# Six attention nodes as one flow of 48 units, with float32r stacks made by the projections

## The chip, the cores and the metric

The kernel runs on one core of one Trainium2 chip. The metric is the device time of one execution in microseconds; the time before is the median of three. The core has five engines that matter here, each working through its own instructions in order: TensorE (PE, with its weight loads shown as PEld), VectorE (DVE), ScalarE (ACT), GpSimd (POOL) and SyncE (SP, which issues DMAs). They wait for each other through semaphores.

## The reference, cut to what matters

The whole program is eight sublayers over x of shape (8, 256, 128). Only the feed-forward of layer 0 is touched. It is six attention nodes with heads of 16 elements, each reading up to three earlier nodes:

```python
for c in range(6):
    nsrc = min(c + 1, 5); snode = c - nsrc
    eq, ek, ev = lind + nsrc - 1, lind, lind + nsrc // 2
    q = ew[c, 0] * (nodes[c - 1] @ We[eq] + be[eq])
    k = ew[c, 1] * (nodes[snode] @ We[ek] + be[ek])
    v = ew[c, 2] * (nodes[snode + nsrc // 2] @ We[ev] + be[ev])
    # mha: H = 8 heads; softmax(qh kh^T / sqrt(16)) vh, then @ Wo
    nodes[c] = act_w[c] * mha(q, k, v, Wq[c], Wk[c], Wv[c], Wo[c]) + q
    lind += nsrc
return layernorm(nodes[5], ln_g, ln_b)
```

Batch n of node c reads only batch n of earlier nodes.

## The kernel before, in words

Layer 0's feed-forward is the functions `l0f_*` (lines 748 to 866). `l0f_sp` loads the weights, `l0f_dve` normalises x (`ln_dve`), then for each of the six nodes c there are three stages with a barrier of all five engines between them:

1. Projections, for all 8 batches at once in 512-column chunks: `cols_pe` (L671) makes q with columns as tokens (`qcol`) and, in `tcol`, k; `rows_pe` (L681) multiplies by Wq and Wk and puts rows of tokens into `Qf` and `Kf`; then v goes the same way into V. `l0f_empty` evacuates the banks, alternately on ACT and DVE (L696, L703, L704, L712), and multiplies the edge weight `ew` in at that point.
2. Attention, batch after batch (`Heads.events` gives the order, `att_pool`, `att_pe`, `att_act`, `att_dve` carry it out). There are 4 pairs of heads in a batch. POOL splits the float32 q and k of `Qf` and `Kf` into three bf16 parts each, set side by side in `Qst` and `Kst`, 6 x 16 entries for a head (L281 to L300). PE transposes these stacks (K and T events, L337), ACT and DVE evacuate them (L455, L469). A: PE scores of a pair (L379, contraction over 97 rows), of which DVE takes the row maxima (L479). After each half of the heads DVE writes the negated maxima as two bf16 columns into `Qst` (L489, L491), PE transposes this stack again (X event) and ACT evacuates it as `QpT` (L459). B: PE makes the transposed scores with the maxima in the contraction (L392, 99 rows), ACT takes the exponential (L451). V: PE multiplies by v (L406), O: ACT copies the result (L446), R: PE turns it (L416) and DVE divides by the sum (L501, L504).
3. Output: PE turns O (L663), evacuated into `tcol`; PE multiplies by Wo (L671); DVE makes `nodes` (L819).

Banks 0 and 1 hold the scores of A, 2 and 3 those of B, 4 the product with v. Banks 5 to 7 are taken in turn by everything else (`turning`), and a job waits until the job three before it has been evacuated. A pair's A waits for the maximum of the pair before, its B for the exponential of the pair before.

After the sixth node PE turns the result back (L663) and DVE does a second layer norm (L231 on). The DVE and POOL work at the edges of the stage is in L231 to L237, L253 to L259 and L846. Layer 1's attention (L971 to L1126) and layer 3's feed-forward (L1664 to L1898) are not changed; they already use float32r operands.

## Time and profile before

| | us |
|---|---|
| median of 3 runs | 2422.3 (2419.29 to 2423.67) |
| the profiled execution's own time | 2432.78 |
| its span | 2431.0 |
| layer 0's feed-forward, from its first instruction to the second layer norm | 231.3 to 1074.65 |

| engine | busy us | share of the span |
|---|---|---|
| PE | 1654.4 | 68% |
| PEld | 1154.3 | 47% |
| DVE | 1533.2 | 63% |
| ACT | 948.1 | 39% |
| POOL | 523.8 | 22% |

Busy time is the time in which an engine works on an instruction; waiting for a semaphore is not busy. L12 is line 12 of the kernel. Where a row says what ended an engine's idle time, that is inferred from semaphore events. Times are in us from the start of the span unless marked ns.

### The profile page before, as it was taken

How to read it: one execution, taken by the hardware profiler on the slowest of the kernel's cores; microseconds unless marked ns; L12 is line 12 of the kernel's file. 1: busy time of each engine (PE TensorE's matmuls, PEld its weight loads, DVE VectorE, ACT ScalarE, POOL GpSimd, SP SyncE). 2: the span in 40 equal slices, each digit the busy share in tenths (PEclk: the TensorE clock that was granted, in tenths of full speed). 3: DMA queues.
4: the chain of work that ended last, by engine and by line, in shares of the span. 5: the costliest groups of instructions: out<-in, count | busy, mean ns of one | idle time of the engine just before them, and what ended most of it. 6: DMA issues, size and time to landing. Idle time of an engine off the chain costs nothing. (4 is left out here: it accounts for less than half of the span.)

```text
span 2431.0 us, 39616 instructions
## 1 busy us (share of the span) xinstructions
PE 1654.4 (68%) x16146; PEld 1154.3 (47%) x16146; DVE 1533.2 (63%) x2306; ACT 948.1 (39%) x1175; POOL 523.8 (22%) x746
## 2 busy tenths in 40 slices
PE   1784787887877787853898889334882367630598
PEld 0562555555565555531565556223651334320497
DVE  5664563656556563666666766685658767569565
ACT  0563473755547473741333333122662047510010
POOL 6321341415143341401000000014300233000121
PEclk9997898999989998985999999756996669855599
DMA  1013000000000000001000000000000000000143
GB/s 56 4 10 73 3 1 1 1 1 2 1 1 1 1 1 1 1 1 53 1 1 1 1 1 1 9 20 1 2 2 9 26 1 1 18 34 17 38 125 103
DMA packets 61355, 38.28 MB, mean 16 GB/s; under 512 B 37572, under 2 KB 53380, under 8 KB 60420
## 3 DMA queue, kind: packets, MB, share of 16 engines
q1 hardware_dynamic: 60164, 34.55, 5.1%
q8 instruction: 127, 2.08, 0.4%
q0 software_dynamic: 1024, 1.32, 0.2%
q14 instruction: 40, 0.33, 0.0%
HBM read 32.71 MB, written 3.15 MB: 15 GB/s over the span
## 5 line engine op out<-in xcount | busy, mean ns | idle before, releaser
L451 ACT ACTIVATE Pt<-bank 128x1024 f32<-128x1024 f32 (+1 forms) x384 | 366.3, 954 | 302.7 <-PE bank L392 301.5
L479 DVE TENSOR_REDUCE Mx<-bank 128x4 f32<-128x1024 f32 x256 | 312.8, 1222 | 101.9 <-PE bank L379 101.7
L379 PE MATMUL bank<-KT,QT 97*128 97x256 bf16 (+2 forms) x1536 | 198.1, 281 | 87.1 <-DVE Mx L479 70.5
L392 PE MATMUL bank<-QpT,KT 99*128 99x256 bf16 (+2 forms) x1536 | 186.8, 267 | 37.1 <-ACT QpT L459 33.5
L406 PE MATMUL bank<-Pt,V 128*32 128x256 f32 (+1 forms) x3072 | 198.9, 378 | 9.6 <-ACT Pt L451 9.6
L337 PE MATMUL bank<-identb,Qst 128*128 128x128 bf16 x2304 | 174.8, 232 | 19.2 <-POOL Qst L300 14.1
L455 ACT COPY QT<-bank 128x1024 bf16<-128x1024 bf16 x144 | 139.4, 1027 | 112.1 <-PE bank L337 112.1
L469 DVE COPY KT<-bank 128x1024 bf16<-128x1024 bf16 x144 | 98.8, 691 | 132.7 <-PE bank L337 132.4
L281 POOL CAST Kst<-Kf 128x256 bf16<-128x256 f32 x72 | 28.6, 398 | 706.8 <-PE bank L337 403.2
L337 PE MATMUL bank<-identb,Kst 128*128 128x128 bf16 x1152 | 94.6, 233 | 117.9 <-POOL Kst L290 68.5
L459 ACT COPY QpT<-bank 128x1024 bf16<-128x1024 bf16 x144 | 145.0, 1007 | 72.6 <-PE bank L337 72.6
L337 PEld LDWEIGHTS bank<-identb,Qst 128*128 128x128 bf16 x2304 | 150.7, 104 | 39.9 <-issue 16.5
L379 PEld LDWEIGHTS bank<-KT,QT 49*128 49x128 bf16 (+1 forms) x1536 | 89.5, 98 | 163.4 <-DVE Mx L479 84.9
L392 PEld LDWEIGHTS bank<-QpT,KT 51*128 51x128 bf16 (+1 forms) x1536 | 107.5, 98 | 69.7 <-ACT QpT L459 47.9
L337 PEld LDWEIGHTS bank<-identb,Kst 128*128 128x128 bf16 x1152 | 74.2, 105 | 135.4 <-issue 69.6
L406 PEld LDWEIGHTS bank<-Pt,V 128*32 128x32 f32 x3072 | 81.6, 111 | 84.1 <-issue 40.1
L501 DVE RECIPROCAL Rden<-bank 128x16 f32<-128x16 f32 x96 | 24.8, 258 | 146.6 <-PE bank L416 146.6
L1120 DVE RECIPROCAL st<-bank 128x256 f32<-128x256 f32 x64 | 111.9, 1749 | 7.8 <-PE bank L1033 7.7
L663 PE MATMUL bank<-ident,Qf 128*128 128x128 f32 x64 | 14.3, 415 | 148.6 <-POOLq L162 96.1
L1095 DVE TENSOR_TENSOR qk_lo<-bank,qk_hi 128x512 fp32r<-128x512 f32 x64 | 44.1, 689 | 102.5 <-ACT qk_hi L1064 102.5
L1190 POOL MEMSET top<- 128x1 f32 x2 | 0.2, 99 | 493.8 <-PEq L162 493.8
L476 DVE TENSOR_REDUCE Mx<-bank 128x2 f32<-128x256 f32 x128 | 54.4, 425 | 81.0 <-PE bank L379 77.0
(331 smaller groups left out, 3576.7 us busy)
## 6 DMA issues: line engine op xcount, KB each, us to landing
Wup<-in_L_upT SPq DMA_DIRECT2D x16, 512.0 KB, 3.6
Wdn<-in_L_downT SPq DMA_DIRECT2D x16, 256.0 KB, 3.7
Aup<-in_L_aupT SPq DMA_DIRECT2D x16, 128.0 KB, 3.7
s_rows<-XG SPq DMA_DIRECT2D x1, 1032.0 KB, 8.1
tA<-in_x_heads SPq DMA_DIRECT2D x1, 1024.0 KB
ctxS<-in_ctx_heads SPq DMA_DIRECT2D x1, 1024.0 KB
s_heads<-O SPq DMA_DIRECT2D x16, 64.0 KB, 4.0
w_kv<-in_L_xattn_w_kv SPq DMA_DIRECT2D x1, 1024.0 KB
```

The source lines that it names most:

```text
L337: last = pe.transpose(bank16[b][:, u * P:(u + 1) * P], src(u), identb[:, :])
L379: last = pe.matmul(bank[x][:, t * S:t * S + w], QT[rs, n % 2, u, t * P:(t + 1) * P], KT[rs, n % 2, u, 0:w], start=(not L.causal and t == 0 ...
L392: last = pe.matmul(bank[2 + x][:, t * S:t * S + S - q0], KT[rs, n % 2, u, t * P:(t + 1) * P], QpT[rs, u, q0:S], start=(not L.causal and t ...
L406: last = pe.matmul(bank[4][32 * x:32 * x + 32, c + q0:c + S], Va[:, 2 * n + k, 4 * i + x, :], Pp[:, (f + x // 2) % 4, x % 2, k * S:k * S + ...
L451: act.activation(Pp[:, g % 4, :, 0:w], banks[:, 2:4, 0:w], ACT.Exp, scale=L.scale).then_inc(exp_done, 1)
L455: act.copy(QT[:, n % 2, :, i * P:(i + 1) * P], bank16[place[kind, n, i]].rearrange("p (u q) -> p u q", u=8)).then_inc(tpT_free, 1)
L459: act.copy(QpT[:, 4 * i:4 * i + 4, :], bank16[place[kind, n, i]].rearrange("p (u q) -> p u q", u=4)).then_inc(tpX_free, 1)
L469: d.tensor_copy(KT[:, n % 2, :, i * P:(i + 1) * P], bank16[place[kind, n, i]].rearrange("p (u q) -> p u q", u=8)).then_inc(tpK_free, 1)
L476: d.tensor_reduce(Mx[:, 0, hs], banks[:, 0:2, 0:P], AX, ALU.max)
L479: d.tensor_reduce(Mx[:, :, hs].rearrange("p t h -> p h t"), banks[:, 0:2, :].rearrange("p h (t k) -> p h t k", t=2), AX, ALU.max).then_inc ...
L1095: d.tensor_tensor(qk_lo[:, r, j, :], bank[5], qk_hi[:, r, j, :].bitcast(F32), ALU.subtract).then_inc(lo_done, 1)
L1120: d.reciprocal(st1[:], y[:, S:2 * S]).then_inc(pair_done, 1)
```

## The change

The six nodes become one flow of 48 units (unit u is batch u % 8 of node u // 8), with no barrier between nodes. `Flow.events` gives the order: in step s, PE, ACT and DVE work at the same time on the projections of unit s+2 (S and Y), the scores and maxima of unit s+1 (A, N), the exponentials and products of unit s (B, V, O), and the end of unit s-1 (R, T, U).

- We is folded into Wq and Wk ahead of each node (W events: `wst`, a stationary of 4 x 128 columns in which each head's 16 columns stand three times, kept as float32r high part and rest, with the edge weight multiplied in). S: three float32r products (high by high, high by rest, rest by high) of `wst` with the node's columns give for two heads a stack of q or k directly; ACT writes one part of its rows with a scale by row (`rowk`), DVE writes projection minus that into the same place. POOL splits the node's columns into high part and rest (`parts`). So the bf16 splits, the transposes K, T and X, and their evacuations are gone.
- The contraction is now over 49 and 50 rows, one head in each half of the rows, where it was 97 and 99.
- The negated maxima are turned by PE (N, 2 small transposes), copied by DVE to `NMrow`, and put by a DMA of SP as rows into the stack: two for each unit, 96 in all.
- Y makes v with one product (We times Wv, folded), T and U make the output and the new node for one batch, on ACT.
- Ahead of the flow `l0f_sp` issues 17 loads where it was 10, and POOL scales the output weights with 12 multiplications.

Sizes and names of buffers that lie elsewhere in memory are left out of the diff here.

```diff
+class Flow:
+    def __init__(self, dh, causal, units, node):
+        self.dh, self.causal, self.units, self.node = dh, causal, units, node
+        self.H = D // dh
+        self.per = self.H // 4
+        self.slot = P // self.per
+        self.pad, self.top = 3 * dh, 3 * dh + 1
+        self.pairs, self.outs = self.H // 2, self.H // 8
+        self.scale = float(dh) ** -0.5
+    def rows(self, h, n):
+        r = self.slot * (h % self.per)
+        return slice(r, r + n), h // self.per
+    def events(self):
+        half, step = self.pairs // 2, self.pairs // 4
+        out = [("W", 0, k) for k in range(3)] if self.node else []
+        def ok(u):
+            return 0 <= u < self.units
+        for s in range(-2, self.units + 1):
+            w, a, b, f = s + 2, s + 1, s, s - 1
+            for j in range(self.pairs):
+                if ok(a):
+                    out.append(("A", a, j))
+                if ok(b):
+                    out.append(("B", b, j))
+                if j == 0 and ok(b):
+                    out.append(("N", b, 1))
+                if j == half and ok(a):
+                    out.append(("N", a, 0))
+                if j == 1 and ok(f):
+                    out.append(("R", f, self.outs - 1))
+                if self.outs == 2 and j == 5 and ok(b):
+                    out.append(("R", b, 0))
+                if self.node and j >= 2 and ok(f):
+                    out.append(("T" if j == 2 else "U", f, 0))
+                if j == 0 and ok(f):
+                    out += [("V", f, half - 1), ("O", f, self.outs - 1)]
+                elif j > 0 and j % 2 == 0 and ok(b):
+                    out.append(("V", b, j // 2 - 1))
+                    if j == 4:
+                        out.append(("O", b, 0))
+                if j % step == 0 and ok(w):
+                    out.append(("S", w, j // step))
+                if self.node and j == 3 and ok(w):
+                    out.append(("Y", w, 0))
+                if self.node and j == 2 and ok(b) and b // B < 5 and b % B in (2, 3, 4):
+                    out.append(("W", b // B + 1, b % B - 2))
+        return out
...
+        wst = sb("wst", [P, 2, 2, 2, 512], F32R, scope=s1)
+        bst = sb("bst", [P, 2, 2, 4], scope=s1)
+        lb = sb("lb", [P, 2, 2, 4], scope=s1)
+        bv = sb("bv", [P, 2], scope=s1)
+        parts = sb("parts", [P, 2, 2, 2, S], F32R, scope=s1)
+        QS = sb("QS", [P, 3, 4, S], F32R, scope=s1)
+        KS = sb("KS", [P, 3, 4, S], F32R, scope=s1)
+        Mf = sb("Mf", [P, 2, 2, 2, 8], scope=s1)
+        NMf = sb("NMf", [P, 2, 2, 2, 8], scope=s1)
+        NMrow = sb("NMrow", [8, 4, S], F32R, scope=s1)
...
+        def flow_sp(s, L):
+            e = s.eng
+            for kind, u, j in L.events():
+                if kind == "N":
+                    e.wait_ge(nmax_out, 2 * u + j + 1)
+                    e.dma_start(QS[L.top:P:L.slot, u % 3, 2 * j:2 * j + 2, :].bitcast(F32),
+                                NMrow[0:2 * L.per, (2 * u + j) % 4, :].bitcast(F32)).then_inc(top_in[j], 16)
+        def flow_pool(g, L):
+            e = g.eng
+            for kind, u, j in L.events():
+                if kind == "W" and j == 0:
+                    if u > 0:
+                        e.wait_ge(w_full, 3 * u)
+                    for k in range(2):
+                        d4 = wd[:, k].rearrange("p (h s d) -> p h s d", s=4, d=L.dh)[:, :, 0:3, :]
+                        w4 = Wn[:, k, u].rearrange("p (h d) -> p h d", d=L.dh).unsqueeze(2)
+                        e.tensor_copy(d4, bc(w4, [P, L.H, 3, L.dh])).then_inc(wd_in, 1)
+                elif kind == "S" and j % 2 == 0:
+                    c, n = u // B, u % B
+                    if c > 0:
+                        e.wait_ge(u_done, u - B + 1)
+                    if u >= 2:
+                        e.wait_ge(stk_full, 4 * (u - 2) + j + 2)
+                    node = nodes[:, NODES[c][1 - j // 2][1], n * S:(n + 1) * S]
+                    hi, lo = parts[:, u % 2, j // 2, 0], parts[:, u % 2, j // 2, 1]
+                    e.tensor_copy(hi, node).then_inc(parts_in, 1)
+                    e.wait_ge(parts_in, 4 * u + j + 1)
+                    e.tensor_tensor(lo, node, hi.bitcast(F32), ALU.subtract).then_inc(parts_in, 1)
...
+                elif kind == "S":
+                    b = turning(kind, u, j)
+                    if n == 0:
+                        pe.wait_ge(w_done, 3 * c + 3)
+                    pe.wait_ge(parts_in, 4 * u + 2 * (j // 2) + 2)
+                    k = 1 - j // 2
+                    hi, lo = parts[:, u % 2, j // 2, 0], parts[:, u % 2, j // 2, 1]
+                    for i in range(2):
+                        m = slice((2 * (j % 2) + i) * P, (2 * (j % 2) + i + 1) * P)
+                        for f in range(3):
+                            w, x = ((0, hi), (0, lo), (1, hi))[f]
+                            last = pe.matmul(b[:, i * S:(i + 1) * S], wst[:, c % 2, k, w, m], x, start=(f == 0),
+                                             stop=(f == 2), skip_group_check=True)
+                    last.then_inc(stk_full, 1)
...
+                elif kind == "A":
+                    if j == 0:
+                        pe.wait_ge(stk_done, 4 * u + 4)
+                    if g > 0:
+                        pe.wait_ge(max_done, g)
+                    for t in range(2):
+                        for x in range(2):
+                            rs, k = L.rows(2 * j + x, L.top)
+                            last = pe.matmul(bank[x][:, t * S:(t + 1) * S], QS[rs, u % 3, k, t * P:(t + 1) * P],
+                                             KS[rs, u % 3, k, :], start=(t == 0), stop=True, skip_group_check=True)
+                    last.then_inc(sm_full, 1)
...
+                    if j % (L.pairs // 2) == 0:
+                        pe.wait_ge(top_in[j // (L.pairs // 2)], 16 * (u + 1))
+                    if g > 0:
+                        pe.wait_ge(exp_done, g)
+                    for t in range(2):
+                        for x in range(2):
+                            rs, k = L.rows(2 * j + x, L.top + 1)
+                            last = pe.matmul(bank[2 + x][:, t * S:(t + 1) * S], KS[rs, u % 3, k, t * P:(t + 1) * P],
+                                             QS[rs, u % 3, k, :], start=(t == 0), stop=True, skip_group_check=True)
+                    last.then_inc(st_full, 1)
...
+                elif kind == "T":
+                    b = turning(kind, u, j)
+                    pe.wait_ge(norm_done, 2 * (Ub + u + 1))
+                    for t in range(2):
+                        last = pe.transpose(b[:, t * P:(t + 1) * P], O[:, 2 * n + t, :], ident[:, :])
+                    last.then_inc(t_full, 1)
+                elif kind == "U":
+                    b = turning(kind, u, j)
+                    pe.matmul(b[:, 0:S], WeS[:, c, :], nodes[:, c, cols], start=True, stop=False)
+                    pe.wait_ge(t_done, u + 1)
+                    pe.matmul(b[:, 0:S], Wn[:, 3, c, :], attT[:, u % 2, :], start=False, stop=True).then_inc(u_full, 1)
...
+                elif kind == "S":
+                    b = bank[place[kind, u, j]]
+                    if n == 0 and j == 0:
+                        act.wait_ge(w_done, 3 * c + 3)
+                    act.wait_ge(stk_full, 4 * u + j + 1)
+                    k = 1 - j // 2
+                    dst = QS if k == 0 else KS
+                    for i in range(2):
+                        m = 2 * (j % 2) + i
+                        last = act.activation(dst[:, u % 3, m, :], b[:, i * S:(i + 1) * S], ACT.Identity,
+                                              scale=rowk[:, k:k + 1], bias=lb[:, c % 2, k, m:m + 1])
+                    last.then_inc(stk_hi, 1)
...
+                if kind == "A":
+                    d.wait_ge(sm_full, g + 1)
+                    r0, k = (2 * j) % L.per, 2 * j // L.per
+                    m = Mf[:, u % 2, k // 2].rearrange("p t (r i) -> p r t i", i=2)[:, r0:r0 + 2, :, k % 2]
+                    d.tensor_reduce(m, banks[:, 0:2, :].rearrange("p h (t k) -> p h t k", t=2),
+                                    AX, ALU.max).then_inc(max_done, 1)
+                    if (j + 1) % half == 0:
+                        i = j // half
+                        d.wait_ge(max_done, g + 1)
+                        d.tensor_scalar(NMf[:, u % 2, i, :, 0:2 * L.per], Mf[:, u % 2, i, :, 0:2 * L.per], -1.0, None,
+                                        ALU.mult).then_inc(nmax_in, 1)
+                elif kind == "N":
+                    b = bank[place[kind, u, j]]
+                    d.wait_ge(nmax_full, 2 * u + j + 1)
+                    d.tensor_copy(NMrow[0:2 * L.per, (2 * u + j) % 4, :], b[0:2 * L.per, 0:S]).then_inc(nmax_out, 1)
+                elif kind == "S":
+                    b = bank[place[kind, u, j]]
+                    d.wait_ge(stk_hi, 4 * u + j + 1)
+                    k = 1 - j // 2
+                    dst = QS if k == 0 else KS
+                    for i in range(2):
+                        m = 2 * (j % 2) + i
+                        x = dst[:, u % 3, m, :]
+                        last = d.scalar_tensor_tensor(out=x, in0=b[:, i * S:(i + 1) * S],
+                                                      scalar=bst[:, c % 2, k, m:m + 1], in1=x.bitcast(F32),
+                                                      op0=ALU.add, op1=ALU.subtract)
+                    last.then_inc(stk_done, 1)
...
         def l0f_pe(p):
-            L = attentions[1]
-            loaded(p, 10)
+            loaded(p, 17)
             p.barrier()
             transposes_pe(p, lambda t: Qf[:, t, :])
-            for c in range(6):
-                (eq, nq), (ek, nk), (ev, nv) = NODES[c]
-                cols_pe(p, We[:, eq, :], nodes[:, nq])
-                cols_pe(p, We[:, ek, :], nodes[:, nk])
-                rows_pe(p, qcol, Wn[:, 0, c, :])
-                rows_pe(p, tcol, Wn[:, 1, c, :])
-                cols_pe(p, We[:, ev, :], nodes[:, nv])
-                rows_pe(p, tcol, Wn[:, 2, c, :])
-                p.settle()
-                p.barrier()
-                att_pe(p, L, bases[1 + c])
-                p.barrier()
-                transposes_pe(p, lambda t: O[:, t, :])
-                cols_pe(p, Wn[:, 3, c, :], tcol, who="DDDD")
+            p.settle()
+            p.barrier()
+            flow_pe(p, L0f, bases[1])
+            p.barrier()
             transposes_pe(p, lambda t: nodes[:, 0, t * P:(t + 1) * P])
             p.barrier()
-        def l0f_empty(seat, me, c, second):
-            if not second:
-                k = 3 * c
-                empty(seat, me, put_affine(seat, me, qcol, ew[:, k:k + 1], ewbe[:, k:k + 1]))
-                empty(seat, me, put_affine(seat, me, tcol, ew[:, k + 1:k + 2], ewbe[:, k + 1:k + 2]))
-                empty(seat, me, put_plain(seat, me, flat(Qf)))
-                empty(seat, me, put_plain(seat, me, flat(Kf)))
-                seat.eng.drain().then_inc(qk_ready, 1)
-                empty(seat, me, put_affine(seat, me, tcol, ew[:, k + 2:k + 3], ewbe[:, k + 2:k + 3]))
-                empty(seat, me, put_v(seat, me, attentions[1]))
-            else:
-                empty(seat, me, put_plain(seat, me, tcol))
-                def node(ci, b):
-                    o = slice(ci * 512, (ci + 1) * 512)
-                    return seat.eng.scalar_tensor_tensor(out=nodes[:, (c + 1) % 6, o], in0=b,
-                                                         scalar=actw[:, c:c + 1], in1=qcol[:, o],
-                                                         op0=ALU.mult, op1=ALU.add)
-                empty(seat, me, node, who="DDDD")
```

## Rows read from the trace of the kernel before

**Rows 1.** The page, part 1: busy us, share of the span, number of instructions.

```profile
span 2431.0 us, 39616 instructions
PE 1654.4 (68%) x16146; PEld 1154.3 (47%) x16146; DVE 1533.2 (63%) x2306; ACT 948.1 (39%) x1175; POOL 523.8 (22%) x746
```

**Rows 2.** Windows: stretch, length, busy us (count) of PE, PEld, DVE, ACT, POOL; PEclk, DMA, GB/s.

```profile
231.00:248.80 17.80, 0.00 (x0) 0.00 (x0) 15.51 (x32) 1.50 (x2) 9.65 (x7) 0.50 0.66 171
248.80:274.00 25.20, 24.32 (x136) 18.39 (x136) 10.39 (x14) 9.35 (x14) 2.91 (x5) 0.94 0.00 1
274.00:378.00 104.00, 80.52 (x908) 56.48 (x908) 63.96 (x94) 66.44 (x71) 42.70 (x67) 0.93 0.01 1
378.00:1075.00 697.00, 558.65 (x5421) 392.23 (x5420) 397.10 (x581) 384.59 (x436) 228.09 (x360) 0.94 0.01 1
```

**Rows 3.** Tile qcol (min/median/max ns, first and last start); then the timeline at the end.

```profile
L703 ACT ACTIVATE qcol<-bank,ewbe,ew x12: 777/777/780, 253.0 to 939.8; 128x512 f32<-128x512 f32 x12
...
1074.65 2.29 DVE L231 TENSOR_REDUCE st<-Qf 128x16 f32<-128x2048 f32 x1
```

**Rows 4.** Windows: one batch of the first node's attention, from maximum to maximum.

```profile
320.42:332.11 11.69, 9.63 (x118) 6.81 (x117) 8.24 (x14) 8.32 (x9) 5.73 (x9) 1.00 0.01 1
```

**Rows 5.** ACT by line and form: count, busy us, mean ns of one, idle before.

```profile
L451 ACT ACTIVATE Pt<-bank 128x1024 f32<-128x1024 f32 x256 | 262.4, 1025 | 199.5 <-PE bank L392 198.2
L446 ACT COPY OT<-bank 128x512 f32<-128x512 f32 x96 | 56.3, 586 | 12.4 <-PE bank L406 12.0
L459 ACT COPY QpT<-bank 128x1024 bf16<-128x1024 bf16 x144 | 145.0, 1007 | 72.6 <-PE bank L337 72.6
L703 ACT ACTIVATE tcol<-bank,ewbe,ew 128x512 f32<-128x512 f32 x24 | 18.7, 778 | 23.9 <-PE bank L671 23.9
L1076 ACT COPY outT<-bank 128x256 f32<-128x256 f32 x8 | 3.0, 372 | 40.7 <-PE bank L1041 40.7
```

**Rows 6.** DVE by line and form.

```profile
L479 DVE TENSOR_REDUCE Mx<-bank 128x4 f32<-128x1024 f32 x256 | 312.8, 1222 | 101.9 <-PE bank L379 101.7
L489 DVE TENSOR_SCALAR Qst<-Mx 128x8 bf16<-128x8 f32 x96 | 32.7, 340 | 3.3
L501 DVE RECIPROCAL Rden<-bank 128x16 f32<-128x16 f32 x96 | 24.8, 258 | 146.6 <-PE bank L416 146.6
L504 DVE TENSOR_TENSOR O<-bank,Rden 128x256 f32<-128x256 f32 x48 | 20.4, 425 | 1.7
L1126 DVE SCALAR_TENSOR_TENSOR X<-bank,g,X 128x256 f32<-128x256 f32 x8 | 3.8, 476 | 4.7 <-PE bank L1047 4.7
```

**Rows 7.** Timeline: PE in order of issue, at full clock; start us, us, what.

```profile
318.09 1.07 PE L406 MATMUL bank<-Pt,V 128*32 128x256 f32 x16
319.09 0.66 PE L416 MATMUL bank<-ident,OT 128*128 128x128 f32 x4
319.58 0.60 PE L379 MATMUL bank<-KT,QT 97*128 97x256 bf16 x4
...
390.57 7.03 PE L671 MATMUL bank<-nodes,We 128*128 128x512 f32 x16
...
1307.99 0.28 PE L1019 MATMUL bank<-qk_hi 64*128 64x256 f32 x2
1308.10 0.28 PE L1019 MATMUL bank<-qk_lo,qk_hi 64*128 64x256 f32 x2
...
2341.97 2.11 PE L1697 MATMUL bank<-sel,yb 80*128 80x512 f32 x8
```

**Rows 8.** DMA issues by line: KB each, median us from issue to landing.

```profile
s_heads<-O SPq DMA_DIRECT2D x16, 64.0 KB, 4.0
xg<-s_rows,sloti POOLq DMA_INDIRECT x32, 2.6
```

**Rows 9.** Windows near the end of the loads; then POOL by line and form.

```profile
245.00:247.00 2.00, 0.00 (x0) 0.00 (x0) 1.97 (x2) 0.00 (x0) 0.00 (x0) 0.50 0.00 0
...
L290 POOL TENSOR_TENSOR Kst<-rest,Kst 128x256 bf16<-128x256 f32 x72 | 49.6, 689 | 5.8
```

More of the change, by code:

```diff
@@ L75, in events, with banks @@
         return out + [("R", B - 1, last)]
+class Flow:
[45 more added lines that the diff above has]
+        return out
+    def banks(self):
+        turns = [e for e in self.events() if e[0] in "NSRTUYW"]
+        return {e: 5 + k % 3 for k, e in enumerate(turns)}
 def flamingo(nc, T, out):
@@ L511, in flamingo @@
             bases.append({"N": nb_, "P": pb_, "U": ub_})
-            nb_, pb_, ub_ = nb_ + B, pb_ + B * L.pairs, ub_ + B * L.halves
+            if L is L0f:
+                pb_, ub_ = pb_ + L.units * L.pairs, ub_ + L.units * L.outs
+            else:
+                nb_, pb_, ub_ = nb_ + B, pb_ + B * L.pairs, ub_ + B * L.halves
         x_rows = T["x"].rearrange("b (t p) c -> p (b t) c", p=P)
@@ L760, in l0f_sp @@
+            loads += [(WeS[:, c], T["L0_ffn_We"][NODES[c][0][0]]) for c in range(6)]
+            for dst, src in loads:
                 e.dma_start(dst, src).then_inc(dma_in, 16)
-            s.count("in", 10)
+            s.count("in", 17)
             s.barrier()
-            for c in range(6):
-                s.barrier()
-                s.barrier()
+            s.barrier()
+            flow_sp(s, L0f)
+            s.barrier()
             s.barrier()
         def l0f_pool(g):
-            L = attentions[1]
@@ L770, in l0f_pool @@
-            stack_fill(g, L)
-            g.count("in", 10)
+            e = g.eng
+            e.memset(wd, 0.0)
+            e.memset(V[:, 0:NT * L0f.H * 32], 0.0)
+            g.link(e.memset(rest[:], 1.0))
+            g.link(e.tensor_copy(v_view(L0f)[:, :, :, L0f.dh:L0f.dh + 1], bc(rest[:, 0:1].unsqueeze(1).unsqueeze(1),
+                                                                           [P, NT, L0f.H, 1])))
+            loaded(g, 17)
+            for c in range(6):
+                e.tensor_tensor(WeS[:, c], WeS[:, c], bc(ew[:, 3 * c:3 * c + 1], [P, D]), ALU.mult)
+                g.link(e.tensor_tensor(Wn[:, 3, c], Wn[:, 3, c], bc(actw[:, c:c + 1], [P, D]), ALU.mult))
@@ L824, in l0f_act @@
         def l0f_act(a):
             rstd_act(a, NT)
-            loaded(a, 10)
+            loaded(a, 17)
             a.barrier()
             empty(a, "A", put_plain(a, "A", nodes[:, 0]))
-            for c in range(6):
-                l0f_empty(a, "A", c, False)
-                a.barrier()
-                att_act(a, attentions[1], bases[1 + c])
-                a.barrier()
-                l0f_empty(a, "A", c, True)
+            a.barrier()
+            flow_act(a, L0f, bases[1])
+            a.barrier()
@@ L1434, in x_pool @@
         def x_pool(g, k):
-            L = attentions[5 + k]
+            L = attentions[k]
             stack_fill(g, L)
@@ L1444, in x_pool @@
             g.barrier()
-            att_pool(g, L, bases[5 + k], padf if k == 2 else None)
+            att_pool(g, L, bases[k], padf if k == 2 else None)
             g.barrier()
@@ L2036 @@
     laid["ctxT"] = _np.ascontiguousarray(laid["ctx_1024"].reshape(-1, D).T)
+    laid["L0_WeT"] = _np.ascontiguousarray(laid["L0_ffn_We"].transpose(2, 0, 1))
     laid["beT"] = _np.ascontiguousarray(laid["L0_ffn_be"].T)
```

288 lines of the change are left out of this document (227 added, 61 removed).

## Prediction

> **What bounds the kernel now.** I read the page's shares of busy time first [rows 1]: no engine is busy for more than 68% of the span, so what a change is worth has to be read stage by stage. The stretches of layer 0's feed-forward come next [rows 2]: 17.8 us of loads and layer norm with PE idle, 25.2 us of projections of a node, in which PE is busy for 24.3 us, and some 104 us of attention, in which PE is busy for 80.5, ACT for 66.4 and DVE for 64.0. Node follows node at (939.8 - 253.0) / 5 = 137.4 us [rows 3]; six make 824 us, a third of the span. Then I read one batch in the middle of an attention [rows 4]: it takes 11.69 us at full clock, and no engine fills it (PE 9.63, ACT 8.32, DVE 8.24). It is bounded by waits handed round: of the stacks' turn through POOL, PE and ACT, and of banks 5 to 7. Eight such batches are 93.5 us; the other 44 us of a node are projections, ramps at the barriers, and the output. So a unit (a batch of a node) costs 137.4 / 8 = 17.2 us today. That is the number that a unit of the flow has to beat.
>
> **The change part by part, for one unit.** Durations are from [rows 5 to 7].
>
> ACT. Taken away: four evacuations of stacks at 1.007, half of the projections' evacuations. What remains or comes: 4 exponentials at 1.025 = 4.10; O 0.586; S, 8 activations of 128x256 with a scale and a bias. No row has this form: 128x512 with both takes 0.778, a plain copy of 512 takes 0.586 and of 256 0.372, so 0.778 - 0.214 = 0.564 each, 4.51 in all. Y is a plain copy, 0.372. T and U have a bias only: between 0.372 and 0.564, I take 0.468 each, 0.94. Sum 10.51. W is 2 x 0.778 a node, 0.19 a unit.
>
> DVE. Removed: K evacuations and bf16 maxima. Now: 4 maxima at 1.222 = 4.89; S, 8 operations of 128x256 from PSUM with a tensor and a scalar, at 0.476 as in L1126 = 3.81; 2 copies of the turned maxima (few partitions, same 256 columns) at no more than 0.425 = 0.85; reciprocal and product 0.258 + 0.425 = 0.68; 2 negations, each 0.2 alone, 0.34 in the mean beside POOL [rows 6]. Sum 10.63 to 10.91. W is 2 operations of 512 and 6 small ones a node, about 2.8 us, 0.35 a unit.
>
> PE at full clock. S: 24 float32r products with 256 moving columns. With 80 rows in use and 512 columns, 8 of them last 2.11 with the tail of 0.2, so 0.24 each and 0.12 for 256 [rows 7]: 2.8. A and B: 16 each, two heads in the two halves of the rows. In layer 1 a pair with 64 rows each issues 0.11 to 0.12 after the pair before (1307.99, 1308.10) [rows 7], so 8 pairs make 0.94 for A and 0.94 for B, where four matmuls over 97 rows took 0.44 an event. V as before, 2 x 1.0 (318.09 to 319.09). R 0.49, T 0.23, N four transposes at 0.12, 0.47. U: two float32 products of 256; 8 of 512 took 7.03, so 0.44 each, 0.9. Y 0.47. W about 4 us a node, 0.5. Sum 9.7.
>
> POOL: two copies and two subtractions, at most 0.69 each, 2.8 against 5.73 now [rows 4, 9]; it works two units ahead and hides. SP: two DMAs a unit, nothing else is in its queue; each stands between DVE's copy and a B on PE.
>
> So three engines need 10 to 11 us each where nothing but order ties them. The unit takes more than the largest of them. I laid one step out in the order of `events`, each engine in its own order, a PE result 0.2 after its last issue (the tail above), banks 5 to 7 released three jobs later. With the first maximum of a step as time 0, DVE runs: A0 0 to 1.22, N 1.64, then it waits until 2.35 for ACT's S0 (ACT has had the exponential and O ahead of it); S0 3.30, A1 and negation 4.76, R 5.44, S1 6.39, A2 7.61, N 8.03; a wait until 8.73 for ACT's S2, behind T and the product S2, which PE could only issue once S1 had left its bank; S2 9.68, A3 and negation 11.1; a wait to 11.35, S3 12.30. The period is **12.3 us**: 10.65 of DVE's work and 1.65 of three waits for ACT. For the negations lengthened by POOL I add 0.15.
>
> The DMAs in this schedule have 3.1 to 3.2 us from the end of the copy to the point at which PE wants the row. The trace has no transfer within SBUF and none as small (4 KB). The nearest rows bound it from above: 2.6 for the gather of rows, 4.0 for 64 KB in 32-byte pieces to DRAM [rows 8]; from below, the wait can be nothing. I take the lower row, since four pieces of 1 KB are nearer to it, so the cost is 0; at 4.0 it is 0.8 us twice a unit.
> The trace has its shortest landing at 2.6. The Trainium skill (DMA: Bandwidth & Descriptors, "Anatomy of one DMA") puts the fixed part of a DMA at about 2.0 us; by that the row would be hidden too, as an estimate, and no run here shows this size yet.
>
> A second cost that I put near nothing is DVE against POOL. The mean of the small negation is 0.34 with POOL at work, while L504, which reads PSUM, takes 0.425 on the mean, though it runs beside POOL [rows 6]. S has the second pattern, one operand from PSUM and one from SBUF. Should each of POOL's four operations hold DVE for its whole length, that is up to 2.8 a unit; I keep it as an end of the range.
> The Trainium skill (SBUF — State Buffer, "SBUF: two separate sides") says that DVE and GpSimd lock a shared port pair when DVE runs in a two-port mode or has two operands in SBUF; S has neither, so by the rule the term is 0.
>
> **The sum.** Head: loads end before 245 [rows 9]. They grow from 10 to 17, with 0.4 MB more; about 3 us of issue, so they end near 247, inside the layer norm (to 248.8). POOL's 12 multiplications of 128x128 (half of L290's 0.689, with its overhead 0.4) are a chain of 4.8 behind them, to about 252: **+3.6**. Transposes, a barrier, then POOL's spread, W and its evacuation, 3.0 + 1.4 + 6.2: the first S at 263. Before, the projections began at 252. Fill: steps -2, -1 and 0 at 6.4, 9.5 and 11.5 (four times ACT's S; four times maximum and S; no end of a unit). Full steps: 45 x 12.3 = 553.5, and 5 x 3.1 = 15.5 for W. Drain: 8.5, 7.6 and 5.7. That is 263 + 27.4 + 569 + 21.8 = 881. The last transposes and copies take 4.0 and a barrier 0.3, so the second layer norm begins at 885.7, where it was 1074.65 [rows 3]: **189 us less**. With the negations' 0.15 x 46 = 7, 182 less. The execution that was profiled had 2432.8 (span 2431.0), so it would be 2251; the median stands 10.5 below it: 2422.3 - 182 = **2240 us**. PE's clock: it stands at 0.93 in an attention with its barriers and at 1.00 inside one [rows 2, 4]. The flow has no barrier, so I reckon with 1.00; at 0.93 PE's 9.7 become 10.4, still below DVE.
>
> **The rivals.**
> 1. The rows of maxima come late. If they land 4.0 after issue, each B that opens a half holds PE, with V and S behind it, for 0.8: 1.6 a unit, 46 units, +74: 2314. For it: 4.0 stands in the trace, and PE can't go past a waiting B. Against: the size, and 2.6. Chance 0.17.
> 2. The waits for ACT close up and only the busiest engine counts: 11.0 with W instead of 12.3 + 0.35 + 0.15, so 46 x 1.8 = 83 less: 2157. Against: today's batch of 11.69 leaves 2 us unused on its fullest engine [rows 4], with the same rings of banks. Chance 0.08.
> 3. The steps are longer than by hand, because DVE's S is held by POOL, or because 49 and 50 float32r rows in two halves don't go side by side (then A and B cost 1.9 more on PE, of which 1.3 fits into PE's idle time): about +1 a unit, 46: 2286. Against: 64 rows do go side by side in layer 1, and L504 isn't lengthened. Chance 0.19.
> 4. The flow doesn't do what it says, and stalls at each change of node: POOL's parts of the next node wait for U of eight units before, and the new weights for W. If each of five changes drains and fills, 5 x 20 = 100: 2340. Against: U of that unit is five steps old when S needs it, W ends five steps ahead. Chance 0.04.
> 5. Slower than before. One mechanism: the DMA of the maxima. Each unit has two in its path; the flow loses when a unit exceeds 12.3 + 182 / 46 = 16.3, that is when each row lands 2.0 past its slack, 5.2 us or more after the copy. Only large transfers come near that. At 6.0 it would be 2 x 2.8 x 46 = 258 more: 2498. Chance 0.02.
>
> **How the numbers follow.** The forecast holds 0.50, with a range of its own of 2200 to 2280. It and rivals 1 and 3 make up 0.86, rival 2 lies below, 4 and 5 above. The range from 2185 to 2325 leaves out most of 2, all of 4 and 5, and a little of the rest: 0.8. A measurement of this kernel tells 0.2%, some 5 us, from no change. All but rival 5 are faster by far more: faster 0.97, same 0.01, slower 0.02.
>
> **What would show it.** In the profile after: from one first maximum of a unit to the next 12 to 13 us; DVE busy for about 10.9 of it, ACT 10.7, PE near 10; DVE's waits named as ACT's S, not SP. S on ACT 0.56, on DVE 0.48; A and B issuing in 0.24. The DMA of a row landing in 2 to 3 us, and B with no wait for it. The second layer norm at about 890. Wrong would be: PE waiting for a DMA ahead of B (rival 1), S on DVE near 0.7 (rival 3), A over 0.4, a gap every eighth unit (rival 4), or ACT's activation of 256 far off 0.56, which counts eight times.

## The result and the profile after

The changed kernel takes 2338.5 us in the median of four runs (2333.1 to 2344.8) against 2423.0 (2419.3 to 2423.7): a ratio of 0.965 (0.963 to 0.967), 84.5 us less. The forecast was 2240 with a range from 2185 to 2325; the direction was right, the gain was less than half of it.

The page's first lines, of the kernel after; its execution took 2333.1 us:

```profile
span 2331.2 us, 37487 instructions
...
PE 1576.6 (68%) x14945; PEld 1116.7 (48%) x14946; DVE 1556.4 (67%) x2522; ACT 961.6 (41%) x1439; POOL 367.0 (16%) x527
```

DVE is at 67% where it had 63% [rows 1]: more work in less time, still not full. Where the time went is read from the start of the second layer norm, the row that answers to 1074.65 [rows 3]:

```profile
995.22 2.29 DVE L315 TENSOR_REDUCE st<-Qf 128x16 f32<-128x2048 f32 x1
```

It starts 79.4 us earlier. The spans of the two profiled executions differ by 99.8 us; the other 20.4 lie in stages whose instructions are the same in both (layer 1's attention was 7.5 us shorter, the last feed-forward 7.8, the stages between them the rest), and the two profiled executions stand on opposite sides of their medians: 2432.8 is 10 above, 2333.1 is 5 below. So the change is worth 79 us in its stage, where I had worked out 182 to 189. From this row to the end of the program the same work took 1336 to 1356 us in the eleven profiled executions of this case (1356.3 before, 1336.0 after), so what an edit is worth in the stage is read from this row as well as from the time of the whole.

The head and the flow in windows (length; busy us and count of PE, PEld, DVE, ACT, POOL; PEclk, DMA, GB/s), after:

```profile
231.00:256.00 25.00, 3.11 (x15) 3.12 (x16) 17.09 (x21) 2.34 (x4) 13.65 (x16) 0.50 0.48 138
...
290.00:900.00 610.00, 499.52 (x4408) 362.19 (x4406) 414.32 (x770) 396.20 (x657) 95.44 (x172) 0.94 0.01 2
```

Against [rows 2], PE is busy for 82% of the flow, DVE for 68%, ACT for 65%. The granted clock is 0.94 although no barrier is left. These 610 us hold 40 units: 15.2 each, with the new weights of five nodes among them; I had 12.3 and 0.35 for the weights.

The costs of single instructions, by line and form in the flow after (count, busy us, mean ns of one, idle before and what ended it):

```profile
L1074 DVE TENSOR_REDUCE Mf<-bank 128x4 f32<-128x1024 f32 x160 | 195.0, 1219 | 24.1 <-PE bank L958 24.1
...
L1025 ACT ACTIVATE Pt<-bank 128x1024 f32<-128x1024 f32 x159 | 162.8, 1024 | 105.2 <-PE bank L976 103.8
...
L1038 ACT ACTIVATE QS<-bank,lb,rowk 128x256 fp32r<-128x256 f32 x160 | 81.7, 561 | 55.3 <-PE bank L938 51.7
...
L1093 DVE SCALAR_TENSOR_TENSOR QS<-bank,bst,QS 128x256 fp32r<-128x256 f32 x160 | 69.8, 477 | 66.6 <-ACT QS L1038 66.6
...
L1084 DVE CAST NMrow<-bank 4x256 fp32r<-4x256 f32 x80 | 32.1, 402 | 0.0
```

ACT's S takes 561 ns (forecast 564), DVE's 477 (476), the copy of the turned maxima 402 (at most 425). DVE waited 66.6 us ahead of its S on QS alone, for ACT.

Then I followed one unit through the timeline after, from the end of one step into the next (start us, us, what, idle before and releaser). It answers to the batch of [rows 4]:

```profile
504.80 1.02 ACT L1038 ACTIVATE QS<-bank,lb,rowk 128x256 fp32r<-128x256 f32 x2
...
505.38 0.72 POOL L877 TENSOR_TENSOR parts<-nodes,parts 128x256 fp32r<-128x256 f32 x1
505.45 0.67 DVE L1079 TENSOR_SCALAR NMf<-Mf 128x8 f32<-128x8 f32 x1
...
506.04 0.86 DVE L1093 SCALAR_TENSOR_TENSOR QS<-bank,bst,QS 128x256 fp32r<-128x256 f32 x2
...
506.96 0.50 PE L958 MATMUL bank<-KS,QS 49*128 49x256 f32 x4 [1.75 <-DVE QS L1093]
...
507.30 0.40 PE L976 MATMUL bank<-QS,KS 50*128 50x256 f32 x4
507.50 1.23 DVE L1074 TENSOR_REDUCE Mf<-bank 128x4 f32<-128x1024 f32 x1 [0.60 <-PE bank L958]
...
507.74 1.02 ACT L1025 ACTIVATE Pt<-bank 128x1024 f32<-128x1024 f32 x1 [1.66 <-PE bank L976]
...
507.94 1.07 PE L989 MATMUL bank<-Pt,V 128*32 128x256 f32 x16
...
508.94 0.99 PE L938 MATMUL bank<-parts,wst 128*128 128x256 f32 x6
...
513.09 0.50 PE L958 MATMUL bank<-KS,QS 49*128 49x256 f32 x4 [1.18 <-DVE Mf L1074]
...
520.99 0.50 PE L958 MATMUL bank<-KS,QS 49*128 49x256 f32 x4 [1.75 <-DVE QS L1093]
...
521.54 1.23 DVE L1074 TENSOR_REDUCE Mf<-bank 128x4 f32<-128x1024 f32 x1 [0.60 <-PE bank L958]
...
521.98 1.52 PE L989 MATMUL bank<-Pt,V 128*32 128x256 f32 x16
...
523.43 1.65 PE L938 MATMUL bank<-parts,wst 128*128 128x256 f32 x6
```

The first A of a unit on PE (L958) starts at 506.96 and 520.99: **14.03 us** a unit at full clock. Ahead of each PE stood idle for 1.75 us, released by DVE's S on QS, which ends at 506.90; everything behind A0 in PE's order, B0 and V and the next S, shifts with it. Ahead of the third A (513.09) there is a second gap, for a maximum. The last two rows are the same instructions as those at 507.94 and 508.94, and take 1.52 and 1.65 instead of 1.07 and 0.99. The windows of 2 us over that place show why:

```profile
520.00:522.00 2.00, 1.01 (x14) 0.65 (x14) 1.40 (x4) 0.34 (x2) 0.13 (x1) 1.00 0.00 0
522.00:524.00 2.00, 2.00 (x19) 1.02 (x19) 1.08 (x2) 1.25 (x2) 0.00 (x0) 0.61 0.00 0
524.00:526.00 2.00, 2.00 (x14) 1.70 (x12) 0.00 (x0) 1.01 (x3) 0.00 (x0) 0.53 0.01 2
526.00:528.00 2.00, 1.42 (x14) 1.16 (x10) 1.83 (x3) 1.72 (x4) 0.40 (x1) 1.00 0.00 0
```

From 522 to 526 the granted clock is 0.61 and 0.53, that is TensorE at its level of 1.2 GHz for between 3 and 4 us, and the unit lasts 15.5 (521.54 to the next unit's first maximum at 537.06).

### The profile page after: what moved, and what is told of

Same layout as the page of the kernel before. It is cut to its first block and busy times, and to the rows that moved or that the text cites. A ratio compares the mean times of both kernels' runs of the same rounds, so it can differ in the third digit from the quotient of the medians.

```text
span 2331.2 us, 37487 instructions
## 1 busy us (share of the span) xinstructions
PE 1576.6 (68%) x14945; PEld 1116.7 (48%) x14946; DVE 1556.4 (67%) x2522; ACT 961.6 (41%) x1439; POOL 367.0 (16%) x527
## 5 line engine op out<-in xcount | busy, mean ns | idle before, releaser
L1074 DVE TENSOR_REDUCE Mf<-bank 128x4 f32<-128x1024 f32 x192 | 234.1, 1219 | 32.3 <-PE bank L958 32.3
L1025 ACT ACTIVATE Pt<-bank 128x1024 f32<-128x1024 f32 x192 | 196.6, 1024 | 125.6 <-PE bank L976 124.0
L535 ACT ACTIVATE Pt<-bank 128x768 f32<-128x768 f32 (+1 forms) x192 | 169.6, 883 | 134.9 <-PE bank L476 134.2
L938 PE MATMUL bank<-parts,wst 128*128 128x256 f32 x1152 | 207.3, 320 | 1.3 <-DVE bv L1126 1.3
L938 PEld LDWEIGHTS bank<-parts,wst 128*128 128x128 f32 x1152 | 167.6, 207 | 47.4 <-issue 42.1
L958 PE MATMUL bank<-KS,QS 49*128 49x256 f32 x768 | 102.4, 347 | 128.7 <-DVE QS L1093 79.3
L958 PEld LDWEIGHTS bank<-KS,QS 49*128 49x128 f32 x768 | 61.2, 197 | 169.5 <-DVE QS L1093 88.7
L1038 ACT ACTIVATE KS<-bank,lb,rowk 128x256 fp32r<-128x256 f32 x192 | 98.0, 560 | 39.8 <-PE bank L938 38.6
L989 PE MATMUL bank<-Pt,V 128*32 128x256 f32 x1536 | 110.8, 409 | 0.1
L490 PE MATMUL bank<-Pt,V 128*32 128x256 f32 (+1 forms) x1536 | 90.0, 352 | 2.9 <-ACT Pt L535 2.9
L563 DVE TENSOR_REDUCE Mx<-bank 128x4 f32<-128x1024 f32 x64 | 78.2, 1222 | 20.5 <-PE bank L463 20.4
L1420 ACT ACTIVATE Pt<-bank 128x1024 f32<-128x1024 f32 x64 | 65.5, 1024 | 60.6 <-PE bank L1367 60.6
```

Source lines behind the costliest of these rows:

```text
L490: last = pe.matmul(bank[4][32 * x:32 * x + 32, c + q0:c + S], Va[:, 2 * n + k, 4 * i + x, :], Pp[:, (f + x // 2) % 4, x % 2, k * S:k * S + ...
L535: act.activation(Pp[:, g % 4, :, 0:w], banks[:, 2:4, 0:w], ACT.Exp, scale=L.scale).then_inc(exp_done, 1)
L563: d.tensor_reduce(Mx[:, :, hs].rearrange("p t h -> p h t"), banks[:, 0:2, :].rearrange("p h (t k) -> p h t k", t=2), AX, ALU.max).then_inc ...
L938: last = pe.matmul(b[:, i * S:(i + 1) * S], wst[:, c % 2, k, w, m], x, start=(f == 0), stop=(f == 2), skip_group_check=True)
L958: last = pe.matmul(bank[x][:, t * S:(t + 1) * S], QS[rs, u % 3, k, t * P:(t + 1) * P], KS[rs, u % 3, k, :], start=(t == 0), stop=True, ski ...
L989: last = pe.matmul(bank[4][32 * x:32 * x + 32, S * (j % 2):S * (j % 2) + S], Va[:, 2 * n + k, 4 * j + x, :], Pp[:, (f + x // 2) % 4, x % 2 ...
```

## The experiments

In all of them the kernel after is the base. Two theories stood against each other at first. **W**: I had left one wait out of my step, that of the first A for the last S of its own unit. **C**: the granted clock is what costs. Times are medians of four runs, beside runs of the kernel before on the same chip (2422.8 beside e1 to e4, 2422.6 beside e5 to e7, 2421.1 beside e8 and e9).

**The wait loosened (e1_split_wait).** The pair of A0 reads what S0 and S2 have written; S3 is needed only by the third A.

```diff
-                    if j == 0:
-                        pe.wait_ge(stk_done, 4 * u + 4)
+                    if j % 2 == 0:
+                        pe.wait_ge(stk_done, 4 * u + 3 + j // 2)
```

> One wait of PE is loosened: the first A of a unit waits for three of the unit's four S (all that its pair reads), and the third A for the fourth; the result is unchanged. Theory W (my schedule left out that A0 waits for the last S of its unit, and this wait alone makes 14.0 us of 12.3): at full clock a unit falls from 14.03 to 12.3 to 12.7 us, PE no longer waits 1.75 us for DVE's QS ahead of the first A, and the time falls by 1.3 to 1.7 x 46 = 60 to 80 us, to 2260 to 2280. Theory C (the granted clock of PE is what costs, and the order hides the wait): under 20 us less, as the clock of the flow falls below 0.94 when PE is given more to do.

It took 2259.8 us, 78.7 below the kernel after; ratio to before 0.933 (0.930 to 0.935). The timeline of e1 around two unit starts:

```profile
504.38 1.02 ACT L1038 ACTIVATE QS<-bank,lb,rowk 128x256 fp32r<-128x256 f32 x2
...
505.16 0.50 PE L958 MATMUL bank<-KS,QS 49*128 49x256 f32 x4 [0.37 <-DVE Mf L1074]
...
505.63 0.86 DVE L1093 SCALAR_TENSOR_TENSOR QS<-bank,bst,QS 128x256 fp32r<-128x256 f32 x2
...
506.42 1.21 DVE L1074 TENSOR_REDUCE Mf<-bank 128x4 f32<-128x1024 f32 x1
...
517.81 0.51 PE L958 MATMUL bank<-KS,QS 49*128 49x256 f32 x4 [0.37 <-DVE Mf L1074]
...
519.08 1.21 DVE L1074 TENSOR_REDUCE Mf<-bank 128x4 f32<-128x1024 f32 x1
```

A0 (505.16) no longer waits for the S on DVE that starts at 505.63, and the first maxima follow each other at 506.42 and 519.08: 12.66 us a unit. Theory W holds. The second layer norm starts 84.9 us earlier than in the kernel after (995.22):

```profile
910.30 2.29 DVE L315 TENSOR_REDUCE st<-Qf 128x16 f32<-128x2048 f32 x1
```

The whole gained less, since the stages behind it took 1352.3 us in this execution, 16 more than in that of the kernel after. The clock moved as well, against what I wrote for theory C: it rose. The flow from 300 to 850 in one window, after:

```profile
300.00:850.00 550.00, 452.61 (x3970) 327.99 (x3971) 372.84 (x696) 355.71 (x590) 85.15 (x153) 0.94 0.01 2
```

and in e1:

```profile
300.00:850.00 550.00, 485.75 (x4548) 359.13 (x4548) 421.52 (x793) 405.93 (x678) 97.96 (x176) 0.99 0.01 2
```

0.94 became 0.99, with PE busier (486 us instead of 453). So the 86 us by which first to last maximum shrank (706 to 621) are of two kinds: 46 x (14.03 - 12.66) = 63, and some 23 from falls of the clock that no longer happen. Both follow from the one edit; e4 below takes them apart.

**Work in PE's gap (e4_filler).**

```diff
                     if j == 0:
-                        pe.wait_ge(stk_done, 4 * u + 4)
+                        pe.wait_ge(stk_done, 4 * u + 2)
                     if g > 0:
                         pe.wait_ge(max_done, g)
+                    if j == 0:
+                        for _ in range(12):
+                            pe.matmul(bank[0][:, 0:S], wst[:, c % 2, 0, 0, 0:P], KS[:, u % 3, 0, :], start=True,
+                                      stop=True, skip_group_check=True)
+                        pe.wait_ge(stk_done, 4 * u + 4)
```

> Twelve matmuls of 256 columns (1.4 us at full clock) are added on PE ahead of each unit's first A, into the 1.75 us in which PE waits for DVE; they are overwritten and the result is unchanged. Theory C (PE's clock falls when PE is kept busy, and each fall costs): mean granted clock in the flow falls from 0.94 to 0.90 or less and the time rises by 15 to 50 us. Theory F (the falls of the clock don't depend on PE's work): the time stays within 5 us of 2338, since the work fits into idle time.

It took 2324.5 us: 14 **less** than the kernel after, with 12 matmuls more in each unit. Both expectations fell. The window of the flow in e4:

```profile
300.00:850.00 550.00, 495.64 (x4512) 373.59 (x4508) 380.46 (x713) 364.68 (x608) 88.08 (x158) 0.99 0.01 2
```

The clock stands at 0.99. A unit's plain period is 14.22 where it was 14.03 (the filler costs 0.19), yet no plain unit is at 15.5 any more: 46 x 0.19 = 9 more and 14 to 15 less in all leave 23 to 24 us for the falls of the clock, the same figure as in e1. So theory C had the sign wrong: more work on PE, fewer falls.

What stands ahead of each fall can be read from the traces. Between 290 us and the last maximum the kernel after has 18 of them. 15 begin within 2 us of the end of a gap of 1.58 or 1.75 us on PE. The other three come behind the last event of W (new weights), where PE shows no gap but 18 matmuls with a single moving column. In e4 the long gaps are filled, those of 1.2 us remain, and there are three falls, all behind W; in e1 there are four, all behind W, and none behind its 45 gaps of about 1.3. One of these four, in e1:

```profile
447.98 1.84 PE L922 MATMUL bank<-beT,Kf 128*128 128x1 f32 x16
...
448.00:450.00 2.00, 2.00 (x22) 1.99 (x20) 0.88 (x2) 0.88 (x2) 0.00 (x0) 1.00 0.01 2
450.00:452.00 2.00, 2.00 (x12) 1.59 (x12) 1.92 (x7) 1.02 (x1) 0.00 (x0) 0.60 0.00 0
```

So there are two kinds of fall: those behind the long gaps, which e1 and e4 do away with, and those behind W, which stay.

**The DMAs of the maxima left out (e2_no_dma).** `flow_sp` issues nothing, and the wait for `top_in` ahead of B is gone.

> The DMAs of the maxima and PE's wait for them are left out; the transposes and the copies into NMrow stay. The maxima are not subtracted, so the exponentials are others. Theory W: the rows land within the 4.4 us that they have, so the time is the same within 5 us of 2338. Rival D (the rows come late, rival 1 of the prediction): 40 us less or more.

2335.1 us (2331.9 to 2338.8): no difference that can be measured. The 96 rows land in time, and rival 1 is out. The trace of the kernel after shows by how much. A row's copy ends at 509.04, SP issues its DMA at 509.07, and the four packets of 1 KB move within 510.20 to 510.40; nothing moves from then until the B that needs the row, at 513.42:

```profile
510.20:510.40 0.20, 0.20 (x8) 0.20 (x4) 0.00 (x0) 0.20 (x1) 0.00 (x0) 1.00 0.08 21
510.40:513.40 3.00, 1.82 (x18) 1.48 (x16) 2.34 (x5) 2.52 (x5) 1.12 (x2) 1.00 0.00 0
```

From the issue to the end of its last packet a row took 1.30 to 1.46 us, over all 96.

**The flow cut at the nodes (e3_drain).**

```diff
-            return 0 <= u < self.units
-        for s in range(-2, self.units + 1):
+            return lo <= u < lo + B
+        for s in [(B * c, B * c + k) for c in range(6) for k in range(-2, B + 1)]:
+            lo, s = s
```

> The flow is cut at the nodes: each node's eight units run through all steps before the next node's begin; the same work, no barrier. The result is unchanged. Expected if crossing the nodes is what pays: five more drains and fills, 18 us of fill (first S to first B) and 15 us of drain in the trace after, of which a third overlaps what a full step does anyway, 22 us each: 110 more, 2450, slower than the kernel before. Rival (the gain is in the units themselves): under 50 more, still faster than before.

2396.1 us, 58 more than the kernel after: half of what I expected, and still 27 below the kernel before (ratio 0.991, 0.988 to 0.993). From the last unit of a node to the first of the next it is 27.0 us instead of 14 to 15.5, but the next two units are short (10.6 to 12.0 and 13.0 to 14.6), since there is less beside them. The window:

```profile
300.00:850.00 550.00, 447.67 (x3708) 319.07 (x3709) 345.06 (x646) 335.47 (x555) 79.84 (x144) 0.90 0.01 2
```

The clock is at 0.90, the lowest of all, in the run that issued the fewest matmuls there (3708). Part of the 58 us lies outside the stage; the second layer norm starts 45.4 us later than in the kernel after, and 34.0 earlier than in the kernel before:

```profile
1040.65 2.29 DVE L316 TENSOR_REDUCE st<-Qf 128x16 f32<-128x2048 f32 x1
```

Of the 79.4 us that the change is worth in its stage, crossing the nodes thus makes 45, its part in the clock included, and the units and the projections without barriers 34. By the times of the whole it is 58 and 27.

**DVE's negations folded into the copy (e5_split_neg).** On top of e1:

```diff
-                        d.wait_ge(max_done, g + 1)
-                        d.tensor_scalar(NMf[...], Mf[...], -1.0, None, ALU.mult).then_inc(nmax_in, 1)
...
-                    pe.wait_ge(nmax_in, 2 * u + j + 1)
+                    pe.wait_ge(max_done, Pb + L.pairs * u + 2 * j + 2)
...
-                    d.tensor_copy(NMrow[...], b[...]).then_inc(nmax_out, 1)
+                    d.tensor_scalar(NMrow[...], b[...], -1.0, None, ALU.mult).then_inc(nmax_out, 1)
```

> As e1_split_wait, and DVE's two small negations of a unit are folded into its copies of the turned maxima (a multiplication by -1 there). The result is unchanged. Theory W (DVE's order with its waits for ACT sets the 12.66 us of a unit now): 0.20 and 0.67 us of DVE's work go from it, so 0.3 to 0.8 a unit, 14 to 37 us below 2260: 2223 to 2246. Rival E (DVE only waits longer for ACT's S then): under 5 us.

2252.2 us (2246.6 to 2257.6), 8 below e1 with ranges that overlap (e1 2255.7 to 2264.6, in another group of runs). The plain unit goes from 12.66 to 12.61: of 0.9 us of DVE's work taken away almost nothing arrives, and the second layer norm starts at 906.5, 3.8 earlier. The 8 us lie between the two expectations; rival E is right for the step: DVE's waits for ACT's S, 1.33 and 1.28 in e1, become 1.56, 0.43 and 1.44.

**S first in slots 0 and 2 (e6_s_first).** On top of e5, in `events`; for even j the S is now appended ahead of T, U, V and O:

```diff
+                if j % 2 == 0 and ok(w):
+                    out.append(("S", w, j // step))
                 if self.node and j >= 2 and ok(f):
...
-                if j % step == 0 and ok(w):
+                if j % 2 == 1 and ok(w):
                     out.append(("S", w, j // step))
```

> As e5_split_neg, and in slots 0 and 2 of a step the S stands ahead of V, O and of T, V, on every engine. The result is unchanged. Theory W: DVE's waits of 1.3 us for ACT's S in these slots shrink by what V (1.0 on PE) and O or T (0.6, 0.5 on ACT) held them, so 0.5 to 1.2 a unit, 23 to 55 below e5. Rival E (the banks' turn or the exponentials then hold S back by as much): within 10 us of e5, either way.

2231.4 us (2224.8 to 2233.8), ratio to before 0.921 (0.919 to 0.923): the best version, 21 below e5, 107 below the kernel after. The timeline of e6 at the start of a unit:

```profile
499.75 0.97 PE L940 MATMUL bank<-parts,wst 128*128 128x256 f32 x6 [0.60 <-DVE QS L1093]
...
500.65 1.07 PE L991 MATMUL bank<-Pt,V 128*32 128x256 f32 x16
...
500.75 1.02 ACT L1040 ACTIVATE KS<-bank,lb,rowk 128x256 fp32r<-128x256 f32 x2 [0.79 <-PE bank L940]
...
501.81 0.88 DVE L1093 SCALAR_TENSOR_TENSOR KS<-bank,bst,KS 128x256 fp32r<-128x256 f32 x2 [0.67 <-ACT KS L1040]
...
502.60 1.22 DVE L1076 TENSOR_REDUCE Mf<-bank 128x4 f32<-128x1024 f32 x1
...
514.62 1.22 DVE L1076 TENSOR_REDUCE Mf<-bank 128x4 f32<-128x1024 f32 x1
```

The S (L940) now stands ahead of V (L991), ACT's activations begin at 500.75, and DVE's S at 501.81. From first maximum to first maximum (502.60, 514.62) it is 12.02 us. The gain is 0.6 in a plain unit, but the three units with W of a node gain only 0.3, 0.1 and nothing (13.46, 13.29 and 15.96 became 13.17, 13.17 and 16.01), so first to last maximum shrinks by 17 us (619 to 602). Both this and the 21 us of the whole lie below what theory W had (23 to 55) and above the 10 of rival E: the direction was right, the size too large. Now PE's S waits for a bank of the ring, 0.60 us ahead of 499.75. The clock is nearly full:

```profile
300.00:850.00 550.00, 507.86 (x4685) 369.77 (x4683) 408.20 (x731) 420.06 (x700) 99.99 (x179) 0.98 0.01 2
```

**The same without the DMAs (e7_s_first_no_dma).** As e6, with the DMAs and PE's wait left out as in e2.

> As e6_s_first with the DMAs of the maxima and PE's wait for them left out, so that the maxima are not subtracted. It asks whether the row's way is in the path once a unit is shorter. If the rows still land in time, within 5 us of e6; if the 3 us or so that remain for them are too few, 20 to 60 below e6.

2232.6 us (2227.5 to 2241.6), the same as e6, and the same 12.03 a unit. The row's way is hidden even in the shorter unit.

**A and B over 64 rows (e8_rows64, e9_s_first_64).** Both `rows` calls get 64 instead of 49 and 50, in e8 on the kernel after, in e9 on e6.

> A and B contract over all 64 rows of a half of the array instead of 49 and 50 (the rows added hold zeros on one side, so the result is unchanged). In the trace of the kernel after four such matmuls issue in 0.33 us, where layer 1's over 64 rows take 0.22. Theory R (the number of rows makes the difference): 0.22 for A and for B, 0.8 us of PE's work less a unit; as the unit hangs on DVE's S the time changes by 0 to -15 us of 2338, more if the clock changes. Rival K (something else in the operands makes 0.33): it stays at 0.33 and the time at 2338.

> The same edit on top of e6_s_first. Theory R: up to 0.3 of the 12.02 us of a unit, 0 to 15 us below the 2231 of e6. Rival K: 2231.

2333.0 us (2331.4 to 2334.8) and 2227.0 (2223.6 to 2237.0): neither differs from its base beyond the ranges, and the plain units are 14.0 and 12.03 to 12.06 as before. The timeline of e8, a B behind an A:

```profile
505.47 0.50 PE L958 MATMUL bank<-KS,QS 64*128 64x256 f32 x4 [1.75 <-DVE QS L1093]
...
505.81 0.40 PE L976 MATMUL bank<-QS,KS 64*128 64x256 f32 x4
...
506.14 0.38 PE L965 MATMUL bank<-ident,NMf 128*4 128x128 f32 x2
```

Again 0.34 from A's first matmul to B's first and 0.33 on to N's, so the number of rows makes no difference. My premise was a misreading: I had measured layer 1 from weight load to weight load. From matmul to matmul the kernel before has the same there, four in 0.34:

```profile
1311.97 0.50 PE L994 MATMUL bank<-qk_hi 64*128 64x256 f32 x4
...
1312.31 0.28 PE L1019 MATMUL bank<-qk_hi 64*128 64x256 f32 x2
```

Within a longer group a pair follows each 0.11 to 0.12 us; a group of two pairs costs 0.33 with its start. e9 is no faster than e6 beyond the ranges, so I keep e6 as the best version, with e9 its equal.

## Why the prediction was wrong

**The step that failed** is the hand-made step of 12.3 us. In it A0 waited only for the maximum before it, while DVE was still at S3 until 1.40 us later (that maximum ends at 9.68 + 1.22 = 10.90, S3 at 12.30). The code has `stk_done, 4 * u + 4` at j == 0, a wait for the last S of the same unit, which stands one slot earlier. The diff showed it, and I didn't put it in. e1 takes it away and lands at 2260, where the forecast for the whole was 2240.

The second layer norm came at 995.2 instead of 885.7, 109.5 late. By terms:

| term | forecast | measured | over 45 full steps or 5 nodes |
|---|---|---|---|
| wait of A0 for S3 | 0 | 14.03 - 12.66 = 1.37 a unit | 62 |
| the rest of the step | 12.3 | 12.66 (e1) | 16 |
| PE's clock in the flow | 1.00 | 0.94, units of 15.5 among those of 14.0 | 26 |
| new weights (W) of a node | 3.1 | 0.8 + 0.6 + 1.9 = 3.3 (e1, first change of node, no fall of the clock) | 1 |
| head, fill and drain | 263 + 27.4 + 26.1 | first maximum 1.4 later, first two steps 1.9 and 1.5 longer, the end 0.6 | 5 |

They add to 110. Of the clock's 26, 20 are what the 45 steps take longer than in e1 beside the wait (673.4 against 591.7), and 6 are the four falls behind W that e1 still has, 1.5 each: there the third unit with W lasts 16.1, where it is 14.6 at the first change. With the 0.15 a unit for DVE's negations counted in, 7 less is missing.

**The rest of the step.** The order of waits for ACT was right in kind: DVE waits ahead of each S. But in e1 it waits 1.33 in slot 2 and 1.28 in slot 0, where I had 0.70 and 0.71.

**PE's clock.** I took 1.00 from a batch inside an attention [rows 4] and gave "no barrier" as the reason. That batch had PE busy for 82% of its time too; the flow after had gaps of 1.75 and 1.2 us in each unit. e4 shows by an edit that the long gap matters; the falls behind W have no gap ahead of them. What exactly makes the clock fall stays open. The missed wait made this gap too, so most of the clock's term hangs on the same step: with e1's edit the flow stands at 0.99.

**Right.** The head: the first S was forecast for 263:

```profile
263.46 4.69 PE L938 MATMUL bank<-parts,wst 128*128 128x256 f32 x24 [1.31 <-DVE bv L1126]
```

The durations of ACT's and DVE's S. Rival 1 (the row late) was excluded by e2 and e7. The Trainium skill (DMA: Bandwidth & Descriptors, "Anatomy of one DMA") gives a fixed part of about 2.0 us, for DMAs issued from GpSimd. By that figure the row would be hidden, as it is; but these DMAs are issued by SP, and their 1.30 to 1.46 us are below it. Rival 3 has hardly a part in it: A and B take 0.33 instead of 0.24 each, 0.8 us of PE's work a unit, and lie mostly beside DVE's work; the 64 rows of e8 show that it isn't the 49. DVE's S keeps its 477 ns with POOL at work. The negation doesn't: beside POOL's subtraction (505.38 to 506.10) it lasts from 505.45 to 506.12, 0.67 us, where another takes 0.20. The Trainium skill (SBUF — State Buffer, "SBUF: two separate sides") has a lock of the shared ports for DVE operations in a two-port mode. This row is as such a lock would make it; that the negation ran in that mode is not shown. Rival 4 (a stall at each change of node) isn't there: beside the three units with W, the eighth is like the others. Rival 2 was wrong in the same way as the forecast.

The range was too narrow since all its cases took the same hand-made step for granted. An error in the step itself, one wait of 1.4 us times 46, had no place in it.

## What to carry to other kernels

Before a step is laid out by hand, write down every wait of every engine's instructions from the code, also those that say only "all parts of this unit are there"; a wait for the last of four parts, standing right behind the part's producer, undoes the distance that the order seems to give. Such waits are cheap to mend: count which parts the consumer reads, and wait for those. In a flow where the busiest engine has 88% and the other two about three quarters (e1: PE 486, DVE 422 and ACT 406 of 550 us), 0.9 us of work taken off one of them (e5) gave 0.05 a unit, and moving the producer of the late operand ahead of its neighbours (e6) gave 0.6.

Look at what stands ahead of each fall of the clock before counting on a full one: an edit that shortens a wait can be worth more than the wait itself, here 86 us where the wait was 63.

## What the runs showed of the hardware

TensorE's granted clock fell to half for 3 to 4 us, again and again, in a flow with gaps of 1.75 and 1.2 us on PE in each unit. With 12 more matmuls in the longer gap it stood at 0.99, and the kernel became 14 us faster: its four runs (2323.5 to 2326.0) lie below all twelve of the three kernels that have the gap and the same 14.0 us a unit (after, e2, e8: 2331.4 to 2344.8).

Between 290 us and the last maximum the falls stand as follows. Behind gaps of 1.58 to 1.75 us: 15 in the kernel after, 14 in e2, 9 in e8. Behind the 18 one-column matmuls of W, with no gap on PE: 3, 3 and 2 in these, and 4, 3, 4, 5, 4 and 4 in e1, e4, e5, e6, e7 and e9, which have no others. No fall came behind the gaps of 1.2 to 1.3 us that e1, e4 and e5 still have. Not every long gap and not every W is followed by a fall, so neither is the whole condition. Whether the single long gap counts or the idle time in all is not separated: e4 and e1 change both.

In the flow from 300 to 850 the clock was 0.90 in e3, 0.94 in the kernel after and e2, 0.97 in e8, 0.99 in e1 and e4, 0.98 in e6. e8 has the gaps of the kernel after and yet fewer falls. It differs in the rows of A and B, and it ran on another chip than e1 to e7 (chip 9, they on chip 10); these and plain scatter between executions are not told apart. e2 and e4 ran on the same chip.

A DMA of four rows of 1 KB from one place of SBUF to another, issued by SP, took 1.30 to 1.46 us from its issue to the end of its last packet, in each of 96, of which SP spent 0.50 on issuing.
